# Causal attention of the first batch in front of the global maximum, and a new steady order

## The reference, cut to what matters

```python
q_kernel = jnp.exp(h_q + (proj_q - h_q))
k_kernel = jnp.exp(h_k + (proj_k - jnp.max(h_k)))        # over all 32 batches
q_prime, k_prime = nc * (q_kernel + 1e-4), nc * (k_kernel + 1e-4)
# causal: for each token the sums over earlier tokens
out = num / den,   num = sum_j (q'.k'_j) v_j,   den = sum_j (q'.k'_j)
```

## Time and profile before

| | us |
|---|---|
| median of 3 runs | 1069.57 |
| profiled execution | 1069.42 |
| its span, first to last instruction | 1067.6 |
| TensorE busy | 1012.6 (95%) |
| VectorE busy | 961.4 (90%) |
| ScalarE busy | 758.7 (71%) |
| GpSimd busy | 752.5 (70%) |

### The profile page before, as it was taken

How to read it: one execution, slowest core, us unless ns; L and a number is a source line. 1 busy time by engine, 2 the same in 40 slices (tenths; PEclk the granted TensorE clock), 3 DMA queues, 4 the chain that set the end, 5 groups by cost and what they waited for, 6 DMA issues and landing times.

```text
span 1067.6 us, 32201 instructions
## 1 busy us (share of the span) xinstructions
PE 1012.6 (95%) x12870; PEld 831.4 (78%) x12870; DVE 961.4 (90%) x2176; ACT 758.7 (71%) x1564; POOL 752.5 (70%) x1111
## 2 busy tenths in 40 slices
PE   1568999999999999999999999999999999999998
PEld 0447788788888888888888888888888888888787
DVE  7778888999999999999999999999999999998996
ACT  6678877776677777668777666877766687776541
POOL 4578877787677778767778766777876677787531
PEclk9989999999999999999999999999999999999999
DMA  9501000011000001100100100010111000000000
GB/s 311 169 21 31 12 24 29 31 31 31 23 28 25 22 31 31 32 21 24 29 22 32 32 31 22 21 32 21 32 32 31 22 22 31 22 21 12 12 11 30
DMA packets 38915, 38.67 MB, mean 36 GB/s; under 512 B 3440, under 2 KB 38512, under 8 KB 38768
## 3 DMA queue, kind: packets, MB, share of 16 engines
q1 hardware_dynamic: 38384, 36.59, 10.9%
q0 software_dynamic: 384, 0.04, 0.0%
HBM read 28.23 MB, written 8.39 MB: 34 GB/s over the span
## 4 chain that ended last, share of the span: by engine, by line
PE 87%; DVE 5%; POOL 4%; issue 1%; ACT 1%; DMA 0%; SPq 0%; POOLq 0%; DVEq 0%; ACTq 0%
PE ps L2302 15%; PE ps L2304 14%; PE ps L2303 14%; PE ps L2333 10%; PE ps L2348 9%; PE ps L2341 5%; PE ps L2317 5%; PE ps L2382 3%; PE ps L2373 3%; PE ps L2296 2%; PE ps L2358 2%; DVE hk L1770 2%; PE ps L2366 1%; PE ps L2367 1%; PE ps L2325 1%
## 5 line engine op out<-in xcount | busy, mean ns | idle before, releaser
L1434 DVE SCALAR_TENSOR_TENSOR z<-ps,gate,z 128x256 f32<-128x256 f32 x512 | 238.5, 472 | 37.9 <-PE ps L2304 29.0
L2302 PE MATMUL ps<-we_hi,h_hi 128*128 128x512 f32 (+2 forms) x640 | 240.5, 376 | 0.6 <-DVE z L1434 0.4
L2304 PE MATMUL ps<-we_hi,h_lo 128*128 128x512 f32 (+2 forms) x640 | 224.1, 350 | 0.0
L2303 PE MATMUL ps<-we_lo,h_hi 128*128 128x512 f32 (+2 forms) x640 | 223.7, 349 | 0.0
L2302 PEld LDWEIGHTS ps<-we_hi,h_hi 128*128 128x128 f32 x640 | 120.4, 188 | 36.7 <-issue 12.6
L2333 PE MATMUL ps<-qf,kf 64*128 64x256 f32 x1024 | 129.2, 391 | 9.1 <-POOL kf L549 4.5
L2304 PEld LDWEIGHTS ps<-we_hi,h_lo 128*128 128x128 f32 x640 | 120.2, 188 | 17.1
L2303 PEld LDWEIGHTS ps<-we_lo,h_hi 128*128 128x128 f32 x640 | 120.8, 189 | 11.5
L2333 PEld LDWEIGHTS ps<-qf,kf 64*128 64x128 f32 x1024 | 96.4, 191 | 29.8 <-issue 11.3
L2348 PE MATMUL ps<-att,v 128*32 128x256 f32 (+1 forms) x2048 | 109.0, 329 | 3.1 <-POOL att L540 0.9
L911 ACT ACTIVATE att<-ps 128x512 f32<-128x512 f32 x32 | 19.1, 597 | 116.8 <-PE ps L2333 116.7
(11 more groups left out here) (232 smaller groups left out, 3079.7 us busy)
## 6 DMA issues: line engine op xcount, KB each, us to landing
x_in<-in_x SPq DMA_DIRECT2D x32, 256.0 KB, 2.6
c_in<-in_ctx SPq DMA_DIRECT2D x32, 256.0 KB, 2.6
out<-z SPq DMA_DIRECT2D x32, 256.0 KB, 2.2
c_chunk<-in_ctx SPq DMA_DIRECT2D x14, 512.0 KB, 8.0
stage<-in_L_ffn_We SPq DMA_DIRECT2D x2, 1024.0 KB, 10.0
c_chunk<-in_ctx SPq DMA_DIRECT2D x2, 256.0 KB, 6.5
stage_b<-in_L_ffn_bup SPq DMA_DIRECT2D x1, 256.0 KB, 6.9
stage_q<-in_L_ffn_Wq SPq DMA_DIRECT2D x1, 256.0 KB, 6.4
```

The source lines that it names most:

```text
L1434: return dve.scalar_tensor_tensor(out=z[b % 2][:, t, :], in0=ps[:, bank, offset:offset + D], scalar=gate[:, t, ex:ex + 1], in1=z[b % 2][:, ...
L2302: pe.matmul(out, a_hi(c), b_hi(c), start=(c == 0), stop=False)
L2303: pe.matmul(out, a_hi(c), b_lo(c), start=False, stop=False)
L2304: last = pe.matmul(out, a_lo(c), b_hi(c), start=False, stop=(c == C - 1))
```

## The change

1. Batch 0. `pk0` to `pk3` add 1e-4 without alpha, so that batch 0's attention can be made against its own maximum. The numerators and denominators are then put right, with A the part that comes from 1e-4 alone: result = alpha * (made - A) + A. A is 1e-4 times the sum of a query's features (`r_sums`, `r_eps`) times the running sums of the values (`prefix`); `eps_part` multiplies them. `nd_less` and `nd_scaled` do the correction on VectorE; `den` and `o_x` of batch 0 read its result from SBUF.
2. Start orders. Batch 0's attention stands before the maximum in all queues. Some zeroing moves from VectorE to GpSimd, and the loads of Wo, Wg, Wdown and of x of batch 1 move among the chunks of keys. The chunk buffers lie elsewhere in SBUF.
3. The steady slot of each queue has a new order, it is used for n = 5 to 30, and the banks are laid out anew, with the waits that go with it. `fkp` and `fk` stand side by side, as do the expert steps after `hn_t`; `o_tr`, `h2_t0` and `h2_t1` come one slot earlier, behind `nt_t`.

The diff, cut to its core:

```diff
-BANK = dict(stab=0, fk0=6, fk1=4, fk2=3, fk3=7, ...)
+BANK = dict(stab=2, fk0=2, fk1=3, fk2=5, fk3=4, ..., first=2, pf0=1, pf1=0, rs=2)
...
 def pk0_(b):                      # gpsimd; pk1, pk2, pk3 alike
-    if b:
-        last = pool.tensor_scalar(..., KERNEL_EPS, 1.0, ALU.add, ALU.mult)
-    else:
-        last = pool.tensor_scalar(..., alpha[:, 0:1], KERNEL_EPS, ALU.mult, ALU.add)
+    pool.tensor_scalar(tokens_of(kf, 0), tokens_of(kf, 0), KERNEL_EPS, 1.0, ALU.add, ALU.mult)
...
+def prefix_():                    # tensor
+    pe.wait_ge(*at("v1", 0))
+    pe.matmul(ps[:, BANK["pf0"], :], causal[:, :], v1[:, 0, :, :].rearrange(...), start=True, stop=True)
+    pe.matmul(ps[:, BANK["pf1"], :], ones[:, :], v1[:, 0, :, :].rearrange(...), start=True, stop=False)
+    pe.matmul(ps[:, BANK["pf1"], :], causal[:, :], v1[:, 1, :, :].rearrange(...), start=False, stop=True)
+
+def r_sums_():
+    pe.wait_ge(*at("ek0", 0))
+    pe.wait_ge(*at("pq0", 0))
+    pe.wait_ge(*at("sel_half"))
+    for t in range(T):
+        for a in range(PAIRS):
+            last = pe.matmul(ps[:, BANK["rs"], t * H + 2 * a:t * H + 2 * a + 2],
+                             qf[:, a, t * P:(t + 1) * P], sel_half[:, :], start=True, stop=True)
+    last.then_inc(*up("r_sums"))
...
+def r_eps_():                     # scalar
+    act.wait_ge(*at("r_sums"))
+    act.activation(r_first[...], ps[:, BANK["rs"], 0:T * H], ACT.Copy, scale=KERNEL_EPS)
...
+def eps_part_():                  # vector, waits for r_eps
+    for t in range(T):
+        last = dve.tensor_tensor(nd_eps[:, t, :, :], <bank pf t>[:, :, 0:HD + 1], <r_first[:, t] broadcast>, ALU.mult)
+def nd_less_():                   # waits for nt_t of batch 0
+    ... dve.tensor_tensor(nd_first[:, t, :, :], nd(1, t)[:, :, 0:HD + 1], nd_eps[:, t, :, :], ALU.subtract)
+def nd_scaled_():                 # waits for alpha
+    ... dve.scalar_tensor_tensor(out=nd_first[...], in0=nd_first[...], scalar=alpha[:, 0:1], in1=nd_eps[...], mult, add)
...
 def X01_(b):                      # first of the X now
+    if not b: pe.wait_ge(*at("eps_part"))
+    if not b: pe.wait_ge(*at("pk2", b))
 def most_turned_():
-    pe.wait_ge(*at("eq0", 0))
     pe.wait_ge(*at("least"))
+    pe.wait_ge(*at("nt0", 0))
...
 # tensor, slot(n)
-    h2_t1_(n-3) h2_t0_(n-3) mm13_(n-4) dn_(n-1) fq_(n+1) mm1g_(n-3) mm0g_(n-3) o_tr_(n-2) mm12_(n-3) kv0_(n-1) kv1_(n-1)
-    o_(n-2) mm10_(n-3) mm11_(n-3) X00_(n+1) X01_(n+1) Y0_(n+1) Y1_(n+1) X11_(n+1) X10_(n+1) av0_(n+1) s_(n-1) av1_(n+1)
-    mm00_(n-3) mm01_(n-3) hn_t_(n) mm02_(n-3) fkp_(n+2) av2_(n+1) pv_(n-1) av3_(n+1) fk_(n+2) mm03_(n-3) nt_t_(n+1) qq_(n)
+    o_(n-2) mm0g_(n-3) mm1g_(n-3) dn_(n-1) fq_(n+1) mm00_(n-3) mm11_(n-3) mm10_(n-3) kv1_(n-1) kv0_(n-1) mm01_(n-3)
+    X01_(n+1) X00_(n+1) Y0_(n+1) X11_(n+1) X10_(n+1) Y1_(n+1) av0_(n+1) s_(n-1) av1_(n+1) hn_t_(n) mm12_(n-3) mm13_(n-3)
+    mm02_(n-3) mm03_(n-3) av2_(n+1) pv_(n-1) av3_(n+1) fkp_(n+2) fk_(n+2) nt_t_(n+1) o_tr_(n-1) h2_t0_(n-2) h2_t1_(n-2) qq_(n)
 # tensor, start
-    first_turned first_all fkp_0 fk_0 fq_0 most_turned stab_all X00_0 X01_0 Y0_0 X10_0 X11_0 av0_0 Y1_0 av1_0 av2_0 av3_0 fkp_1 ...
+    first_turned first_all fq_0 fkp_0 fk_0 prefix r_sums X01_0 X00_0 X10_0 Y0_0 X11_0 av0_0 av1_0 Y1_0 most_turned stab_all av2_0 av3_0 fkp_1 ...
 # scalar, start
-    ... square_16 eq0_0 eq1_0 eq2_0 ek2_0 ek0_0 ek3_0 eq3_0 alpha we_hi3 xn_1 k_hi_1 x000_0 ...
+    ... square_8 eq3_0 eq1_0 eq2_0 h_t_0 square_9 eq0_0 square_10 ek0_0 ek1_0 square_11 ek2_0 ek3_0 r_eps square_12 square_13
+    square_14 x001_0 x010_0 x000_0 x011_0 square_15 square_16 k_hi_1 x100_0 nt0_0 x110_0 x101_0 x111_0 xn_1 h_hi_1 nt1_0 ... alpha ...
 # vector, start
-    ... key_sums_13 most key_sums_14 key_sums_15 key_sums_16 least stabilizer kept c_t_1 gamma2 we_lo3 less ...
+    ... c_t_1 key_sums_10 key_sums_11 wo_hi eps_part key_sums_12 key_sums_13 key_sums_14 most y00_0 y01_0 key_sums_15 key_sums_16
+    least y10_0 stabilizer y11_0 kept less h_lo_1 h_tr_1 x_t_1 gamma2 c_t_2 nd_less nd_scaled den_0 o_x_0 ...
 # vector, slot(n), its end
-    ... a00_(n-3) y11_(n+1) a01_(n-3) h_lo_(n+3) p_t_(n-1) ht_lo_(n) a02_(n-3) x_t_(n+2) o_tok_(n-1) s_rec_(n-1)
+    ... y11_(n+1) a12_(n-3) p_t_(n-1) a02_(n-3) a13_(n-3) a03_(n-3) ht_lo_(n) o_tok_(n-1) s_rec_(n-1)
```

More of the change, by code:

```diff
@@ L28 @@
 MOST = (CHUNKS - 3) * CH * T
[L31 to L34, removed]
+BANK = dict(stab=2, fk0=2, fk1=3, fk2=5, fk3=4, fq0=6, fq1=7, fq2=2, fq3=0, x000=6, x001=4, x010=1, x011=7,
+            y00=2, y01=1, av0=2, x100=3, x101=0, x110=7, x111=5, y10=4, y11=6, av1=7, nd0=1, nd1=0, ht=3,
+            dn=3, qq=7, kv0=5, kv1=6, s=1, pv0=0, pv1=1, otr=6, o=6, h20=3, h21=5, mm0g=5, mm1g=4, mm00=1,
+            mm01=0, mm02=1, mm03=6, mm10=2, mm11=3, mm12=7, mm13=2, first=2, pf0=1, pf1=0, rs=2)
 class Signal:
@@ L163, in build @@
         c_in = [sb(f"c_in{p}", [P, T, D]) for p in range(2)]
+        x1 = [sb(f"x1_{p}", [P, T, D]) for p in range(2)]
         bn6, mv = sb("bn6", [P, T, 6]), sb("mv", [P, T, 2])
@@ L193, in build @@
         signals = [
[L194 to L207, removed]
+            signal("once_pe0", "first_turned first_all r_sums most_turned stab_all"),
+            signal("pe0", "fk X01 X00 X11"),
+            signal("pe1", "fq Y0 av0 av1 av3"),
+            signal("pe2", "Y1 nt_t"),
+            signal("pe3", "hn_t qq kv1"),
+            signal("pe4", "dn kv0 s"),
+            signal("pe5", "pv o_tr o"),
+            signal("pe6", "h2_t0 mm0g mm00 mm01"),
+            signal("pe7", "h2_t1 mm1g mm11"),
+            signal("pe8", "mm10 mm13"),
+            signal("pe9", "mm12 mm02"),
+            signal("pe10", "mm03"),
+            signal("once_dve0", "first_least sel_h first_most first less_first sel_tok sel_half eps_part least_ least stabilizer kept less gamma2 nd_less nd_scaled wq_hi wdn_hi"),
             signal("keys_dve0", "key_sums"),
@@ L210, in build @@
             signal("dve1", "c_t"),
[L211 to L220, removed]
@@ L221, in build @@
-            signal("dve12", "h2_lo0 a0g a00_ a00 a01_ a01 a02_ a02"),
-            signal("dve13", "a12_ a12 a13"),
-            signal("dve14", "a03"),
-            signal("once_act0", "alpha we_hi3 wg_hi"),
+            signal("dve2", "q_st q_mv q_bn x_t"),
+            signal("dve3", "y01 y10 y11 den_s den_d den o_x g_st g_mv g_bn"),
+            signal("dve4", "y00"),
+            signal("dve5", "ht_lo bqq q_t k_t v_t"),
+            signal("dve6", "d_lo bkv0 smax ssub p_t"),
+            signal("dve7", "bkv1 o_tok s_rec"),
@@ L225, in build @@
+            signal("dve8", "ot_lo y2"),
+            signal("dve9", "h2_lo0 ga gmax gm gsum grec gate a0g a00_ a00"),
+            signal("dve10", "h2_lo1 a1g a10_ a10 a11_ a11"),
+            signal("dve11", "a01_ a01 a02_ a02 a03"),
+            signal("dve12", "a12_ a12 a13"),
+            signal("once_act0", "r_eps alpha tanh we_hi0 we_hi3"),
             signal("keys_act0", "square"),
             signal("act0", "h_hi"),
-            signal("act1", "k_hi h_t ek2"),
-            signal("act2", "xn ek3 eq3"),
```

2768 lines of the change are left out of this document (1328 added, 1440 removed).

## The result

The changed kernel takes 1075.06 us in the median of 11 runs (1072.33 to 1077.53), the kernel before 1069.64 in 11 runs beside it. The ratio is 1.0049 (95% interval 1.0042 to 1.0057): 5.4 us slower, where 1053 was forecast. The profiled execution took 1072.33 us, the lowest of its runs; its span is 1070.6 us. Its span is 3.0 us longer than that of the earlier trace rows, so the profile shows a little more than half of what the median lost.

What follows compares the result with a forecast made beforehand. TensorE, busy 95% of the span, was taken as the bound. From 1069.42 us, less 5.5 for the start, 10 for the steady slots and 0.9 for other batches, it forecast 1053 us, range 1045 to 1066.

Steps and rivals of the forecast that it cites:

- the 0.9 of the other batches: Batches 2 to 6 and the tail: the same neighbours occur in places there, together 0.9 us saved.
- Steady slot, TensorE's own products: TensorE's steady slot: cheaper changes of neighbour save 0.4 us, so 30.8 us a slot and 10 us over 25 intervals.
- GpSimd's ten operations from z0 to pq3, before X01, I walk with 0.2 us of room, an estimate: GpSimd's queue in the steady slot: pq3 is done in time for X01, with 0.2 us of room.
- Rival A: Steady slot: the o_tr chain is late by the 0.4 us won, slot stays 31.2; 1064 us, chance 0.12.
- Rival B: Start: gives nothing, the later maximum takes it, VectorE and ScalarE keep their pace; 1058.5 us, chance 0.14.
- Rival C: TensorE's slot: every change costs 0.11 us, so one fewer gives 0.1 a slot; 1061 us, chance 0.07.
- Rival D: Steady slot: VectorE becomes the bound, its waits sum to 2.9 us, slot 31.9; 1081 us, chance 0.08.
- Start, maximum kept at 41: VectorE in the start: the global key maximum is kept near 41 us, 6 us later than before.
- Idle to 120 us, 41: TensorE in the start: some 41 us idle in the first 120 us, a sign that the forecast is right.
- Start, r_sums 3.5 us: TensorE ahead of the maximum: 16 products of 2 columns, between 1.4 and 3.8 us, taken as 3.5.
- Start, batch 1's X at 52 and 5.5 us gained: Start: batch 1's X products begin at 52 us, 9.5 before 61.54; 5.5 us of that taken as kept.

Runs made afterwards that it cites:

- e1: The changed kernel with GpSimd's pk2, pk0 and pk3 moved ahead of z0 and x1 in the steady slot; 1068.02 us, ratio 0.9978 to the kernel before.
- e2: e1 with, in addition, TensorE's o_tr moved from ahead of h2_t0 to behind h2_t1; 1079.53 us.
- e8: Kernel before with fkp directly ahead of fk, m11 ahead of r2 on GpSimd, and VectorE's a01 behind ht_lo; 1061.75 us, ratio 0.9927.
- e13: e1 with identity products in TensorE's idle start stretches and most prefix and r_sums products left out; 1059.43 us, against 1059.48 with them.
- Filled: Changed kernel with unread identity products in TensorE's idle start stretches, 1067.94 us; the kernel before, filled likewise in its own, 1066.98 us.
- e6: e1 with VectorE's weight work wq_lo, wo_lo and b_kv moved ahead of batch 1's y00; 1062.76 us, ratio 0.994 to the kernel before.
- e15: e1 with unread identity products in two idle TensorE stretches alone, 20 ahead of fq_1 and 22 ahead of X01_1; 1062.66 us.

## Why the prediction was wrong

The 5.4 us come out as 4.4 of clock (7.1 less 2.7) and 1.1 of slot, and nothing is left for the start itself; by ratios and not medians, 5.2 are 3.9 of clock and 1.3 for slot and all else. Against the forecast's 16.4 us of gain, the slot is 11.1 us worse (10 not won, 1.1 lost), the start 9.9 (5.5 not won, 4.4 of clock lost), and the 0.9 of the other batches is missing. So two steps failed, GpSimd's room in the slot and the price of the waits in the start. Step by step:

- **Steady slot, TensorE's own products: right.** fkp and fk took 1.13 us as forecast (528.72 to 529.85), mm12, mm13, mm02 and mm03 4.39 in one run (521.95 to 526.34), which is 12 x 0.2327 + 12 x 0.1175 + 0.08 + 0.09 = 4.37. TensorE's timeline of the changed kernel:
```profile
521.95 0.48 PE L2218 MATMUL ps<-we_hi,h_hi 128*128 128x512 f32 x1
...
526.34 0.86 PE L2264 MATMUL ps<-att,v 128*32 128x256 f32 x16
...
528.72 0.51 PE L2233 MATMUL ps<-k_hi,f_hi 32*128 32x512 f32 x4
...
529.85 1.09 PE L2274 MATMUL ps<-ident,nt 128*128 128x128 f32 x8
```
- **"GpSimd's ten operations from z0 to pq3, before X01, I walk with 0.2 us of room, an estimate": the step that failed.** The room was negative. From y2's start (503.64) to pq3's end (513.53) it is 9.9 us, without a pause over 0.15. I looked for lateness in one slot and asked whether each comes in time. But y2 moves with TensorE, so the room is that of a circle: with those products between X01 and o_tr, a slot shorter than 31.27 was not to be had in that order, and shorter products elsewhere in the slot would only have lengthened the wait. No rival named it. e1 shows it by taking three steps out, 0.33 us a slot.
- **Rival A (the o_tr chain): right in kind, with 0.1 of its 0.4 us.** nt_t and o_tr take 1.49 us where twelve transposes at 0.109 take 1.31; e2 shows 0.1 of that to be the wait for o_n. Behind e1 these 0.18 us are about what stands between 30.94 and 30.8; that the one is the other, no run shows.
- **Rival B (the start gives nothing):** with the clock held that is what came, as far as the intervals tell; that the clock would turn nothing into a loss it did not say.
- **Rival C (one price for each change of neighbours).** e8's 0.24 to 0.27 us a slot is over twice its 0.1, and nearer to the sum over stretches. The reading of the Trainium skill, "TensorEngine Tiling (Array Packing)", section Tiling Modes, as one equal drain for each change is too small here; the trace agrees that a change costs, not that it is all.
- **Rival D (VectorE): refuted.** VectorE is busy for 29.5 us of the slot of 31.27, and from 200 to 1000 us the profile puts no wait of TensorE down to it. Its steps from ot_lo to y2 are a part of the circle all the same.
- **Start, maximum kept at 41: right**, 42.41 us. **Idle to 120 us, 41: right**, 41.2.
- **Start, r_sums 3.5 us: the number right by luck.** They took 3.63, but not because "TensorE is cold there": the whole row ran at full pace in the changed kernel, 0.22 us from one product to the next with a granted clock of 1.00, and where the clock fell (e1, 31.11 us on) one took 0.43, well over the ceiling of 0.24. And the sum priced only them: prefix's three products took 3.63 more (23.33 to 26.96). By e13 neither costs time while the clock is held.
- **Start, batch 1's X at 52 and 5.5 us gained: wrong.** o_x of batch 0 was ready at 51.5, not 48.1: lessening and scaling took 2.3 us where I had 1.6, and den 1.56 where it takes 0.86 in the kernel before. The two pq in front of X01_1 took 1.37 and 1.47 us and not 0.62. Those are sizes. What I left out is that the two waits, 4.7 us ahead of fq_1 and 5.2 ahead of X01_1, would put TensorE at half clock, and what stands behind: 3.55 us for X01_1 and X00_1, 3.2 from fq_2 into qq_0, and VectorE's queue behind both. I wrote "TensorE is cold there" for r_sums and priced nothing by it elsewhere, though X00_1 at 3.77 us stood in the earlier trace rows.
- **Why even at a full clock nothing is left** is open in part. Filled, the changed kernel is 3.6 us ahead at batch 1's X (56.4 against 60.0) and 2.3 ahead at the first of batch 2's X and Y (78.3 against 80.6), but not at batch 7's (228.0 against 225.8, of which 1.9 is only that its slot has less work behind X: 88.0 us from batch 31's X to the end, against 89.9). TensorE's idle time from 60 to 240 us is the same in both, 8.4 and 8.0. The lead goes between batches 2 and 7, whose order was changed as well; a part of it may be the half clock at 112 us. Which steps take it, no run shows.

## What to carry to other kernels

Where an engine's queue waits for something that the bottleneck made a slot earlier, add up the whole circle, not the distance to the next use: if it is longer than the slot that you want, it is the slot, and the cure is to take out of it what is ready anyway. In a start full of waits, price the products behind each wait at half clock too (here they were behind waits of 3 us and more), and look at who stands behind them in other queues. And before you put a gain down to an edit, see in the two traces where the lead begins: e6 and e15 had 2 us of theirs ahead of the first step that they changed.
